# A streamed attention and feed-forward stage: value projection in the heads' PSUM bank, LayerNorm's normalising on ScalarE, and the band mask added by VectorE

## What is computed

```
# six layers; per layer, for each of 4 batches of 256 rows (D = 128, 16 heads of 64, window 32)
h      = shift half of the channels of x by one row
q,k,v  = split(h @ Wqkv[l])                      # 128 -> 3 x 1024
q,k    = l2norm per head, times learned scale, rotary with xpos scale
scores = q @ k.T inside a causal band (own key and the 32 keys before it)
x      = x + softmax(scores + band mask) @ v @ Wo[l]
z      = layernorm(x, other half shifted by one row)
x      = x + (gelu(z @ W1_gate + b) * (z @ W1_up + b)) @ W2[l] + b2
```

## Time and profile before

| | us |
|---|---|
| median of 3 runs | 3021.09 |
| lowest, highest | 3013.13, 3024.06 |
| the profiled execution: its own time | 3015.13 |
| its span, first to last instruction | 3013.1 |
| busy in the span: PE, DVE, ACT, POOL | 2597.0, 1779.4, 1535.5, 1430.8 |
| mean granted TensorE clock (1 is 2.4 GHz) | 0.938 |

### The profile page before, as it was taken

How to read it: one execution, slowest core, us unless ns; L and a number is a source line. 1 busy time by engine, 2 the same in 40 slices (tenths; PEclk the granted TensorE clock), 3 DMA queues, 4 the chain that set the end, 5 groups by cost and what they waited for, 6 DMA issues and landing times. The chain is left out here.

```text
span 3013.1 us, 59098 instructions
## 1 busy us (share of the span) xinstructions
PE 2597.0 (86%) x20009; PEld 1658.7 (55%) x20009; DVE 1779.4 (59%) x3856; ACT 1535.5 (51%) x4987; POOL 1430.8 (47%) x2316
## 2 busy tenths in 40 slices
PE   5999969799989889784799996988888888888886
PEld 3555546455555556553455553656566565656655
DVE  3566665446567545555455556666666666666663
ACT  1455537326557556431255544555556556565553
POOL 0344425104456423100044436777777767777672
PEclk8899989898989999996799998999999999999997
DMA  2000000000000000000000002000101001001000
GB/s 67 1 0 0 0 8 2 20 26 1 5 1 2 4 28 0 6 1 7 27 1 0 0 0 63 23 22 26 34 22 29 22 26 33 19 20 35 26 12 8
DMA packets 45610, 47.13 MB, mean 16 GB/s; under 512 B 11899, under 2 KB 31365, under 8 KB 45382
## 3 DMA queue, kind: packets, MB, share of 16 engines
q1 hardware_dynamic: 45382, 44.18, 5.2%
HBM read 31.05 MB, written 0.52 MB: 10 GB/s over the span
## 5 line engine op out<-in xcount | busy, mean ns | idle before, releaser
L1022 POOL TENSOR_TENSOR l_probs<-l_probs,rowinv 128x512 f32<-128x512 f32 (+2 forms) x256 | 192.4, 772 | 570.9 <-DVE rowinv L1034 570.1
L2229 ACT ACTIVATE net_probs<-bank,net_negmax 128x96 f32<-128x96 f32 x768 | 250.9, 338 | 204.6 <-DVE net_negmax L2373 204.3
L1042 DVE TENSOR_REDUCE negmax<-scores 128x1 f32<-128x508 f32 (+4 forms) x512 | 213.1, 468 | 220.1 <-PE scores L919 180.2
L1022 POOL TENSOR_TENSOR lora_probs<-lora_probs,rowinv 128x508 f32<-128x508 f32 (+1 forms) x256 | 149.5, 617 | 250.7 <-DVE rowinv L1034 250.7
L2297 POOL TENSOR_TENSOR net_probs<-net_probs,net_inverse 128x384 f32<-128x384 f32 x192 | 158.5, 826 | 220.0 <-DVE net_inverse L2349 220.0
L2373 DVE TENSOR_REDUCE net_negmax<-bank 128x4 f32<-128x384 f32 x192 | 106.3, 554 | 246.3 <-PE bank L2078 245.6
L2289 POOL TENSOR_TENSOR net_rope<-net_rope,net_sin_parts 128x512 f32<-128x512 f32 x192 | 243.7, 1269 | 10.8 <-DVE net_sin_parts L2342 10.8
L987 ACT ACTIVATE l_probs<-scores,negmax 128x512 f32<-128x512 f32 (+2 forms) x256 | 139.5, 550 | 167.8 <-DVE negmax L1042 167.1
L124 DVE COPY turned<-flip 128x512 f32<-128x512 f32 (+3 forms) x280 | 163.2, 583 | 74.0 <-PE flip L946 64.5
L2307 POOL TENSOR_TENSOR net_rope<-net_rope,net_head_inv 128x512 f32<-128x512 f32 x192 | 201.1, 1047 | 0.0
L734 DVE TENSOR_REDUCE negmax<-scores 128x2 f32<-128x256 f32 (+2 forms) x192 | 157.8, 822 | 65.9 <-PE scores L642 36.4
(11 more groups left out here) (424 smaller groups left out, 6507.2 us busy)
## 6 DMA issues: line engine op xcount, KB each, us to landing
net_w_qkv<-in_L_ffn_Wqkv SPq DMA_DIRECT2D x12, 768.0 KB, 5.3
net_vals_between<-net_vals SPq DMA_DIRECT2D x48, 192.0 KB, 2.5
net_w_out<-in_L_ffn_Wo SPq DMA_DIRECT2D x6, 512.0 KB, 4.2
net_vals_between<-net_vals SPq DMA_DIRECT2D x48, 64.0 KB, 2.0
moe_w<-in_L_ffn_w13T SPq DMA_DIRECT2D x8, 256.0 KB, 2.7
net_w<-in_L_ffn_W SPq DMA_DIRECT2D x6, 341.0 KB
moe_w<-in_L_ffn_w2T SPq DMA_DIRECT2D x8, 128.0 KB, 2.3
ctx_tok<-in_ctx SPq DMA_DIRECT2D x1, 768.0 KB, 6.4
```

What stands on the lines that cost most here:

```text
L1022: last = nc.gpsimd.tensor_tensor(own, own, rowinv[:, u * tail + w:u * tail + w + 1].to_broadcast([P, k1 - k0]), ALU.mult)
L1042: last = nc.vector.tensor_reduce(negmax[:, u * tail + w:u * tail + w + 1], scores[:, 2 * qt + h, k0:k1], AX.X, ALU.max, negate=True)
L2229: last = nc.scalar.activation(prob_blocks(g)[:, w, :], score_blocks(g)[:, w, :], ACT.Exp, bias=maxima[:, g % 4, w:w + 1], accum_out=sums[: ...
```

## The change

1. The value projection goes to bank 7 (`v_bank`), the one that the heads' sums use, and no longer takes `spare`. Before it PE waits until ACT has stored the heads of group s-4 (`stored`), and before the values it waits until ACT has copied v (`v_copied`).
2. z is normalised by ACT (scale `ln_inv`, bias `ln_shift` = -mean x inverse root). DVE writes -mean (one more small operation in tick 6), POOL multiplies it by the inverse root (one more small operation after the 14), and ACT does the two affine copies in tick 7, behind its exp and its copy of q and k, ahead of `znT`.
3. The band mask is no longer put into the bank by PE. The scores go into the bank with start=True, the first block with 96 keys and not 64. DVE adds the fp32 table to the bank and writes `near` in SBUF; the row maximum and exp read `near`. The add is DVE's own first step, and the maximum waits for it.
4. DVE's third gated slice moves from the end of tick 1 to tick 2, right after the row maximum.

```
-                made = signal("window_made", 5)
+                made = signal("window_made", 4)
...
-                        nc.vector.tensor_copy(window16[:, :], window[:, :]).then_inc(made.sem, 1)
...
-                return (KEYS + DH) * w + (WINDOW, -WINDOW, 0, -WINDOW)[w]
+                return (KEYS + DH) * w + (0, -WINDOW, 0, -WINDOW)[w]
...
-                heads = bank[:, 7, 0:N]
+                heads, v_bank = bank[:, 7, 0:N], bank[:, 7, :]
...
-                def score_blocks(g):
-                    return score_bank(g).rearrange("p (w k) -> p w k", w=BLOCKS)
+                def near_blocks(g):
+                    return near[:, g % 2, :].rearrange("p (w k) -> p w k", w=BLOCKS)
...
-                            take_spare()
-                            nc.tensor.matmul(spare, own, w_qkv[:, 2 * INNER + c * BANK:2 * INNER + (c + 1) * BANK],
+
+                            until(pe, stored, min(G, s - VALUES))
+                            until(pe, v_copied, u)
+                            nc.tensor.matmul(v_bank, own, w_qkv[:, 2 * INNER + c * BANK:2 * INNER + (c + 1) * BANK],
                                              start=True, stop=True).then_inc(v_filled.sem, 1)
-                            held = [(v_copied, u + 1)]
+                            values_in = u + 1
...
-                            until(pe, exped, g - 1)
-                            nc.tensor.matmul(score_bank(g), ident16[:, :], window16[:, :], start=True, stop=False)
+                            until(pe, masked, g - 1)
                             for w in range(BLOCKS):
                                 k0 = max(0, w * QB - WINDOW)
-                                first = w * KEYS + (WINDOW if w == 0 else 0)
                                 for h in range(2):
-                                    last = nc.tensor.matmul(bank[rows_of(h), 4 + g % 2, first:(w + 1) * KEYS],
+                                    last = nc.tensor.matmul(bank[rows_of(h), 4 + g % 2, w * KEYS:(w + 1) * KEYS],
                                                             qk_T[rows_of(h), g % 2, 0, w * QB:(w + 1) * QB],
-                                                            qk_T[rows_of(h), g % 2, 1, k0:(w + 1) * QB],
-                                                            start=False, stop=(w == BLOCKS - 1))
+                                                            qk_T[rows_of(h), g % 2, 1, k0:k0 + KEYS],
+                                                            start=True, stop=True)
...
                             until(pe, stored, g)
+                            until(pe, v_copied, values_in)
...
-                            copy("act", vals[:, m % 3, t, half_cols(c)], spare).then_inc(v_copied.sem, 1)
+                            copy("act", vals[:, m % 3, t, half_cols(c)], v_bank).then_inc(v_copied.sem, 1)
...
-                                last = nc.scalar.activation(prob_blocks(g)[:, w, :], score_blocks(g)[:, w, :], ACT.Exp,
+                                last = nc.scalar.activation(prob_blocks(g)[:, w, :], near_blocks(g)[:, w, :], ACT.Exp,
...
+                            act.wait_ge(ln_shifted.sem, ln_shifted.at(0, n + 1))
+                            for q in range(QT):
+                                own = z[:, QT * b + q, :]
+                                affine("act", own, own, ln_inv[:, q:q + 1], ln_shift[:, q:q + 1]).then_inc(normed.sem, 1)
...
-                            pool.wait_ge(spread_in.sem, spread_in.at(0, n + 1))
+                            pool.wait_ge(spread_in.sem, spread_in.at(0, 2 * n + 2))
                             inverse_root(pool, ln_sum[:, :], LN_EPS, ln_inv[:, :], ln_temp, ln_rooted, ROOT_OPS * n)
+                            pool.wait_ge(ln_rooted.sem, ln_rooted.at(0, ROOT_OPS * (n + 1)))
+                            nc.gpsimd.tensor_tensor(ln_shift[:, :], ln_shift[:, :], ln_inv[:, :], ALU.mult).then_inc(ln_shifted.sem, 1)
...
-                            for q in range(QT):
-                                own = z[:, QT * b + q, :]
-                                nc.vector.tensor_scalar(own, own, meanvar[:, q, 0:1], ln_inv[:, q:q + 1], ALU.subtract,
-                                                        ALU.mult).then_inc(normed.sem, 1)
+                            nc.vector.tensor_scalar(ln_shift[:, :], meanvar[:, 0:QT, 0], -1.0, None, ALU.mult).then_inc(spread_in.sem, 1)
                         g = s
                         if 0 <= g < G:
                             dve.wait_ge(scored.sem, scored.at(0, g + 1))
-                            nc.vector.tensor_reduce(maxima[:, g % 4, :], score_blocks(g), AX.X, ALU.max, negate=True).then_inc(maxed.sem, 1)
+
+                            until(dve, exped, g - 1)
+                            nc.vector.tensor_tensor(near[:, g % 2, :], score_bank(g), window[:, :], ALU.add).then_inc(masked.sem, 1)
+                            dve.wait_ge(masked.sem, masked.at(0, g + 1))
+                            nc.vector.tensor_reduce(maxima[:, g % 4, :], near_blocks(g), AX.X, ALU.max, negate=True).then_inc(maxed.sem, 1)
+                        n = at_tick(s, BOTH + 1, PER, JOBS)
```

More of the change, by code:

```diff
@@ L1813, in l3_ffn @@
                 late = sbl("late", [P, 2, P])
-                window, window16 = sbl("window", [P, 4 * KEYS]), sbl("window16", [P, 4 * KEYS], BF16)
+                window, near = sbl("window", [P, 4 * KEYS]), sbl("near", [P, 2, 4 * KEYS])
                 znT, gelu, acts = sbl("znT", [P, N]), sbl("gelu", [P, 3, N]), sbl("acts", [P, 3, N])
@@ L1836, in l3_ffn @@
                 stream(p, GT, (rope, sin_parts, squares, vals, mid), (w_qkv, w_out, w1, w2, vec), (qk_rows, sines, cosines, sin_table, cos_table),
-                       (head_sums, head_inv, head_temp), (ln_sum, ln_inv, ln_temp), (qk_T, probs, flat_p, maxima, sums, inverse, window16),
+                       (head_sums, head_inv, head_temp), (ln_sum, ln_inv, ln_shift, ln_temp), (qk_T, probs, flat_p, maxima, sums, inverse, window, near),
                        (late, znT, gelu, acts))
@@ L1888, in stream @@
             head_sums, head_inv, head_temp = heads_norm
-            ln_sum, ln_inv, ln_temp = ln
-            qk_T, probs, flat_p, maxima, sums, inverse, window16 = softmax
+            ln_sum, ln_inv, ln_shift, ln_temp = ln
+            qk_T, probs, flat_p, maxima, sums, inverse, window, near = softmax
             late, znT, gelu, acts = ffn
@@ L1908, in stream @@
             copied = {e: signal(f"net_copied_{e}", G // 2) for e in ENG}
+            masked = signal("net_masked", G)
             scored, maxed, exped = signal("net_scored", G), signal("net_maxed", G), signal("net_exped", G)
@@ L1914, in stream @@
             low_moved, late_made, late_moved = signal("net_low_moved", JOBS), signal("net_late_made", JOBS), signal("net_late_moved", JOBS)
[L1915 removed]
+            measured, gathered, spread_in = signal("net_measured", 2 * JOBS), signal("net_gathered", 2 * JOBS), signal("net_spread", 2 * JOBS)
             ln_rooted, normed = signal("net_ln_rooted", ROOT_OPS * JOBS), signal("net_normed", 2 * JOBS)
+            ln_shifted = signal("net_ln_shifted", JOBS)
             z_turned, z_moved = signal("net_z_turned", JOBS), signal("net_z_moved", JOBS)
@@ L2032, in _ @@
                 def _(pe):
-                    held = []
+                    held, values_in = [], 0
                     def take_spare():
@@ L2372, in _ @@
                             dve.wait_ge(scored.sem, scored.at(0, g + 1))
-                            nc.vector.tensor_reduce(maxima[:, g % 4, :], score_blocks(g), AX.X, ALU.max, negate=True).then_inc(maxed.sem, 1)
+                            until(dve, exped, g - 1)
[3 more added lines that the diff above has]
+                        n = at_tick(s, BOTH + 1, PER, JOBS)
+                        if n is not None:
+                            l, b = job(n)
+                            k = GT[2]
+                            if b == 0:
+                                dve.wait_ge(ffn_in.sem, ffn_in.at(l, FFN_LOADS))
+                            dve.wait_ge(both_made.sem, both_made.at(0, n + 1))
+                            dve.wait_ge(gelued.sem, gelued.at(0, n + 1))
+                            nc.vector.scalar_tensor_tensor(acts[0:k, 2, :], spare[0:k, N:2 * N], vec[0:k, 4:5], gelu[0:k, 2, :], ALU.add,
+                                                           ALU.mult).then_inc(gated_up.sem, 1)
                         u = at_tick(s, PROJ, 2, S)
@@ L2416, in _ @@
                             copy("dve", xnT[half:D, b * N + 1:(b + 1) * N], spare[half:D, 0:N - 1]).then_inc(shift_upper.sem, 1)
-                        n = at_tick(s, BOTH, PER, JOBS)
-                        if n is not None:
-                            l, b = job(n)
-                            k = GT[2]
-                            if b == 0:
-                                dve.wait_ge(ffn_in.sem, ffn_in.at(l, FFN_LOADS))
-                            dve.wait_ge(both_made.sem, both_made.at(0, n + 1))
```

(5 more changed lines are left out.)

7 lines of the change are left out of this document (1 added, 6 removed).

## The result

The changed kernel takes 3054.31 us (median of 4 runs, 3045.94 to 3064.91), the kernel before 3022.57 beside it (4 runs). The ratio is 1.0109, with a 95% interval of 1.0067 to 1.0152. I had forecast 3018, no change that can be measured. The time lies at the upper end of the range that I gave (2980 to 3055), and the sign is that of the case to which I gave 0.26.

What follows compares the result with a forecast made beforehand. PE's list was taken to bound the stream. Jobs fall from 47.45 to 46.30 us, plus 1.24 for the clock: 47.54 against 47.79. 6 us gained, 3 lost in the last job: 3021.09 - 3 = 3018, range 2980 to 3055.

Steps and rivals of the forecast that it cites:

- the case to which I gave 0.26: Whole kernel measurably slower: 0.05 from the forecast's own case, 0.16 from slower by the clock, 0.05 from slower by POOL.
- T7 to T0: From scores of tick 7 to scores of tick 0: PE waits 3.3 us for z; 7.00 us, before 5.65.
- T6 to T7: From scores of tick 6 to scores of tick 7: v's projection waits for stored heads; 5.39 us, before 6.74.
- DVE is 0.2 late: Tick 6: DVE measures z only after ACT's copy of z's lower half, which adds 0.2 us before exp.
- slower by POOL: Rival: POOL holds up DVE's add or maximum, 0.7 us at five places; a job takes 3.6 more, 3100 us; chance 0.05.
- Mean 1.24 a job: Behind PE's wait for z: the clock falls in nine jobs in ten, costing 1.24 us a job on average.
- slower by the clock: Rival: each clock fall lasts 6.7 us, not 3.3; slower once a fall costs over 1.5 a job; 3047 us; chance 0.16.
- 0.21 us a tick: PE's list: dropping the mask's matmul, less 0.05 for longer scores, saves 0.21 us a tick, 1.7 a job.
- x 23 jobs: Stream total: 0.25 us gained a job, times 23 jobs, is 6 us gained.
- about 3 us: Last job: without projections on PE, the longer path from scores to exp shows in most ticks; about 3 us lost.
- the clock stays up: Rival: the clock mostly holds through the wait for z, keeping 34 us, less 3: 2990 us; chance 0.22.
- no new waits: Rival: PE runs its own list without new waits, a job of 40 us: 2842 us; chance 0.04.

Runs made afterwards that it cites:

- a_lnsum_warm: The changed kernel without DVE's two small operations behind the measuring of z, and with twelve surplus matmuls before PE's wait for z: 2985.89 us, ratio 0.9893.
- a_mask_back: The changed kernel with the mask as PE's matmul again, and maximum and exp reading PSUM: 2968.68 us, ratio 0.9828.
- a_warm: The changed kernel with twelve surplus matmuls, whose result nobody reads, in front of PE's wait for z in tick 7: 3009.07 us, ratio 0.9961.
- b_v_warm: The kernel before with only the value projection moved to bank 7, plus twelve surplus matmuls ahead of PE's wait for z: 2967.97 us, ratio 0.9836.
- a_z_back: The changed kernel with z normalised by DVE again, ahead of the add of tick 7: 3015.47 us, ratio 0.9980.
- b_mask_only: The kernel before with only the mask's part changed, added by DVE into SBUF: 3095.40 us, ratio 1.0242.
- a_lnsum: The changed kernel without DVE's two small operations behind the measuring of z; POOL takes variance and mean itself: 3018.23 us, ratio 0.9991.
- b_z_only: The kernel before with only z's part changed, normalised by ACT behind exp and the copy of q and k: 3081.93 us, ratio 1.0224.

## Why the prediction was wrong

I had the mechanisms and the waits, and sized the clock and one small operation wrongly. Segment by segment of the job from 2268.90 to 2318.02 (predicted with the clock's 1.24 in T7 to T0):

| | predicted | measured |
|---|---|---|
| V to T6 | 6.62 | 6.69 |
| T6 to T7 | 5.39 | 6.25 |
| T7 to T0 | 8.24 | 8.49 (next job 8.70) |
| T0 to T2 | 9.91 | 10.17 (next job 10.75) |
| T2 to T3 | 7.25 | 7.29 |
| T3 to V | 10.13 | 10.23 |
| job | 47.54 | 49.12 (next 49.91), mean 49.52 |

- **"DVE is 0.2 late" (T6 to T7): the failed step.** The add of tick 6 starts at T6 + 1.90, not T6 + 1.08. I looked at when z can be measured, and not at what the operations between then and the add would fall beside. The add of tick 5, and the exps behind it, come later against PE; DVE's measuring of z waits 0.28 for ACT's copy, and `net_ln_sum` starts at T6 + 0.99 where it started at T6 + 0.17. POOL's long addition has then been under way for 0.38 us. The operation takes 0.93 for 0.17 [the DVE and POOL rows above], and v's projection waits 1.42, where I had 0.8. `a_lnsum_warm` gives the price of the two small operations, 0.93 a job, and its T6 to T7 is 5.29, near my 5.39; `a_mask_back` shows that the operation keeps its 0.17 when the mask's part is undone. The rival "slower by POOL" had the mechanism and the wrong place: I tested the add and the maximum with it, and they stayed at 0.556 and 0.553. The Trainium skill (SBUF — State Buffer, "Who interferes with whom") lists tensor_scalar among the operations that can contend with GpSimd for the pair of ports they share, and says that whoever issues first holds the pair for its whole instruction while the other blocks. The rows agree, at a size of two elements: POOL's addition started first, and `net_ln_sum` ended 0.04 us after it. I had cited this rule and applied it only to the add and the maximum.
- **"Mean 1.24 a job" (the clock): mis-sized.** It costs 1.96. The clock fell about as often as I took it (nine jobs in ten), but every second time for 6.8 us, so the rival "slower by the clock" was half true: its long stretch comes in one job of two. Its threshold, 1.5 us a job, was passed, but it hung on a job of 46.30 with the clock up. That job takes 47.56 (`a_warm`), so any fall that costs over 47.79 - 47.56 = 0.23 us a job turns the change slower.
- **"0.21 us a tick" (the mask off PE): mis-sized.** From q's projection to the scores it is 1.05 now (2299.45 to 2300.50), where mask and projection took 1.2 before, and the scores are longer by 0.05: about 0.1 a tick. How much of that reaches the job isn't shown. When clock and small operations are taken out, 46.63 - 46.30 = 0.33 us a job is left in all, 0.18 of it in T0 to T2 (10.09 in `a_lnsum_warm`).
- The job adds up: 0.72 for the clock, 0.93 for the small operations, and as the remainder 0.33, 1.98 in all, which is 49.52 - 47.54. My forecast was 0.25 a job under the kernel before, so either of the first two would have been enough to turn the sign.
- **"x 23 jobs" and "about 3 us" for the tail.** `net_ln_sum` first starts at 1913.2 before and 1929.5 now, in one and the same job, and at 2868.6 in both; that is 20 jobs before and 19 now. By z's transposes the stream runs for some 20 full jobs; these cost 33.5 of the stage's 35.6 us, so 23 was too many. The start costs 2.8 more than before (I had under 1), and from the last full job to the end the changed kernel is 0.7 shorter, where I had 3 us lost.
- **Right, or nearly:** the add 0.556 (0.55), the exp group 1.45 (1.42, from 2278.65 to 2280.10), z at T7 + 5.02 (5.08), PE's wait for it 3.12 (3.3), ups 1.03 to 1.1 (1.3), the waits for the stored heads in tick 3, 0.51 (0.4 to 1.0), and in tick 1, 0.27 in one job of two (0.45), and that `xnT` and the gated slice never hold v's projection again. ACT's two operations on z take 0.87 (0.92). Two of my own signs told against the forecast: v's wait of 1.42 in tick 7, where I had 0.4 to 1.0, and a job over 48.5 us.
- **The rivals** "the clock stays up" (2990) and "no new waits" (2842) fell. The first has its condition met in `a_warm`, which reads 3009: its job is 47.56 and not 46.30, and 0.93 of the difference is the small operations'.

With the clock up throughout, the parts can be priced from the jobs' lengths. The value projection in bank 7 gives 1.64 (47.45 to 45.81, `b_v_warm`). z on ACT (with part 4, which shows nothing) gives 1.29 on top (45.81 to 44.52, `a_mask_back`), and 1.51 if ahead of exp (44.30). The mask on DVE takes 3.04 back (44.52 to 47.56, `a_warm`), of which 0.77 is the stall of the small operation. That is the whole gain lost, +0.11; the slow clock adds 1.96, against 0.34 before: +1.73 a job.

These prices hold in this order only. With z still on DVE, the mask's part costs 1.50 (45.81 to the 47.31 of `a_z_back` where its clock holds), and z on ACT then costs 0.25 more (to 47.56) instead of giving 1.29. What holds in either order is the sum. The change is slower because the mask's part undoes what the others give, and since its long wait costs PE its clock.

Open is what makes a slow stretch 3.4 or 6.8 us long, and with it why jobs of 49.12 and 49.91 alternate; and whether the small operation is free if it stands elsewhere on DVE, which wasn't tried.

## What to carry to other kernels

When an edit shifts one engine's list against another's, look at every operation on it that sits just ahead of a long one on POOL, the tiny ones too. A wait of PE that is moved or merged is not the same idle time: read the granted clock behind each long wait that the trace has, count how often it fell, and don't take a shorter wait for safe (1.74 us was followed by a fall in `a_z_back`, 1.83 never in the kernel before). A part's price depends on which other parts are in: measure it with the others in place, too. Surplus matmuls in a wait that can't be shortened are worth trying (45 us here), and a DVE operation between scores and exp can cost more than the matmul of PE that it replaces.

## What the hardware did that I had not expected

- A `tensor_scalar` on 128x2 elements took 0.17 us in the kernel before, where it came ahead of a POOL operation of 1.27, and 0.89 to 0.93 behind that operation's start, ending when that one ended: in all jobs of the changed kernel but the last two, and so in `b_mask_only`.
- The length of a wait alone doesn't decide whether the clock falls. One of 2.41 us was followed by a fall in some jobs of `a_mask_back` and not in others, two to nine jobs in a row; one of 1.74 in 15 of 21 jobs of `a_z_back`; one of 3.12 us did nothing in one job of the changed kernel (behind z at 2732.20 the clock reads 1.00, and the next job came after 47.58 us), and one of 3.11 nothing in several of `a_lnsum`.
- The slow stretch around the end of the same 3.12 us wait was 3.4 us and 6.8 us long in turn, job after job.
- In `b_z_only` v's projection of tick 3 took 1.23, 1.32, 1.42, 1.54, 1.64, 1.74 us and so on up to 2.08, in jobs that follow each other, each behind the same wait of 2.04: the fall came 0.1 us earlier from job to job. It isn't tied to the end of the wait.
- The unchanged stages ahead took 14.4 us longer in one profiled execution than in the other.
